# Seven edge tiles beside six node groups in a round of stage 1, and a ring of seven edge buffers

## The reference, cut to what matters

```python
# x: 50000 nodes x 256, float32; src, dst: 12500 edges, dst ascending; edge_attr: 12500 x 256
h   = relu(layernorm(x))
agg = zeros.at[dst].add(relu(h[src] + edge_attr))     # sum over the edges of a node
t   = (h + agg) @ W1 + b1                             # 256 -> 512
t   = batchnorm over the 50000 nodes, relu, @ W2      # 512 -> 256
...                                                   # two normalisations over all nodes
x   = x + (h + relu(...))
h   = relu(layernorm(x))
x   = x + relu(h @ W + segment_sum((h @ M)[src], dst))
```

## Time and profile before

| | us | what it is |
|---|---|---|
| median of three runs | 2451.24 | 2449.91 to 2452.41 |
| span of the profiled execution | 2446.4 | first to last instruction |
| PE busy | 2354.5 | 96% of the span |
| DVE busy | 2052.5 | 84% |
| ACT busy | 1713.3 | 70% |
| POOL busy | 1708.5 | 70% |
| stage 1 | 0 to 438 | first load of stage 2 issued at 438.44 |

### The profile page before, as it was taken

The page is one execution under the profiler, slowest core; times in us unless marked ns, Lnnn a source line. Parts: engine busy times, 40 slices in busy tenths (PEclk is TensorE's granted clock), DMA queues, the critical chain, the costliest instruction groups (busy, mean ns, idle before and its releaser), DMA issues. The chain is left out here.

```text
span 2446.4 us, 48745 instructions
## 1 busy us (share of the span) xinstructions
PE 2354.5 (96%) x12271; PEld 2013.5 (82%) x12271; DVE 2052.5 (84%) x5707; ACT 1713.3 (70%) x3449; POOL 1708.5 (70%) x1599
## 2 busy tenths in 40 slices
PE   7999998799999999999999999979999999989997
PEld 6888886588888888888888888858989888969996
DVE  8999997598888888888888888967777777749996
ACT  6999997466666666666666666638888888846664
POOL 5777777577767667767766666717777777767774
PEclk8999999899999999999999999999999999999999
DMA  8888995323444444444444344349999999765662
GB/s 257 283 278 275 278 277 170 124 58 127 152 150 158 163 151 147 146 146 166 153 147 145 145 164 154 141 173 405 405 411 413 413 413 413 294 197 162 173 177 88
DMA packets 242978, 531.73 MB, mean 217 GB/s; under 512 B 53856, under 2 KB 141177, under 8 KB 231442
## 3 DMA queue, kind: packets, MB, share of 16 engines
q1 hardware_dynamic: 182434, 459.36, 51.2%
q0 software_dynamic: 59808, 70.24, 10.2%
q10 hardware_dynamic: 592, 0.54, 0.1%
HBM read 340.23 MB, written 286.84 MB: 256 GB/s over the span
## 5 line engine op out<-in xcount | busy, mean ns | idle before, releaser
L1020 POOL DMA_INDIRECT ar<-sum_table,idx x392 | 462.3, 1179 | 177.6 <-issue 96.5
L1067 ACT ACTIVATE r<-pair,bnC,bnA 128x512 f32<-128x512 f32 x392 | 305.9, 781 | 380.2 <-PE pair L1268 377.7
L1471 POOL DMA_INDIRECT x1d_table<-x1r,slot x392 | 383.8, 979 | 139.8 <-issue 123.9
L1175 DVE CAST rH<-r 128x512 fp32r<-128x512 f32 x392 | 391.0, 997 | 97.7 <-ACT r L1067 97.7
L1694 PE MATMUL pair<-Ws,h1T 128*128 128x256 f32 x1568 | 358.7, 382 | 8.9 <-DVE orr L1602 7.4
L1694 PEld LDWEIGHTS pair<-Ws,h1T 128*128 128x128 f32 x1568 | 290.2, 190 | 52.1 <-issue 14.3
L1284 PE MATMUL bank<-rH,W2h 128*128 128x512 f32 (+1 forms) x784 | 305.6, 390 | 1.8 <-ACT yr L1081 1.8
L1284 PE MATMUL bank<-rL,W2h 128*128 128x512 f32 (+1 forms) x784 | 305.7, 390 | 0.0
L1284 PE MATMUL bank<-rH,W2l 128*128 128x512 f32 (+1 forms) x784 | 305.0, 389 | 0.0
L836 PE MATMUL bank<-hr 128*128 128x257 f32 (+1 forms) x1568 | 274.2, 329 | 9.6 <-ACT hr L535 9.6
L1184 DVE TENSOR_TENSOR rL<-r,rH 128x512 fp32r<-128x512 f32 x392 | 271.1, 691 | 13.5
(11 more groups left out here) (239 smaller groups left out, 5234.1 us busy)
## 6 DMA issues: line engine op xcount, KB each, us to landing
xr<-in_x SPq DMA_DIRECT2D x186, 512.0 KB, 3.9
xy_kept<-xy_table SPq DMA_DIRECT2D x57, 1024.0 KB, 20.7
x_table<-x1r SPq DMA_DIRECT2D x97, 512.0 KB, 19.8
out<-orr SPq DMA_DIRECT2D x97, 512.0 KB
xy_table<-xr SPq DMA_DIRECT2D x89, 512.0 KB, 2.6
xy_table<-yr SPq DMA_DIRECT2D x89, 512.0 KB, 3.3
xyr<-xy_table SPq DMA_DIRECT2D x32, 1024.0 KB, 21.0
sum_table<-e_tot SPq DMA_DIRECT2D x99, 128.0 KB, 4.5
```

The source lines that it names most:

```text
L1020: pool.indirect_dma_start(ar[0:p, s, j, :], None, sum_table[:, :], bass.IndirectOffsetOnAxis(ap=idx[0:p, s, j:j + 1], axis=0), bounds_chec ...
L1067: act.activation(r32[:, m, 0:n], z_ps[m][:, 0:n], ACT.Relu, bias=bnC[:, m:m + 1], scale=bnA[:, m:m + 1]).then_inc(r_kept, 1)
L1175: dve.tensor_copy(rH[:, s, m, 0:n], r32[:, m, 0:n]).then_inc(rh_kept, 1)
L1471: pool.indirect_dma_start(x1d_table[:, :], bass.IndirectOffsetOnAxis(ap=slot[0:p, part, s * T + j:s * T + j + 1], axis=0), x1r[0:p, s, j, ...
```

## The change

A round holds seven steps instead of six. The first six have a group and an edge tile, the seventh an edge tile alone. The number of rounds follows from the tiles, 99 // 7 = 14, instead of from the groups. Every ring of edge buffers and of their semaphores has seven places instead of six, as EU sets them all. Group buffers, AHEAD, the parts of the steps and their instructions are as before.

```diff
-GU, EU = 6, 6
-EH = EU // 2
+GU, EU = 6, 7

 def mixed_rounds(eng, group, edge, group_flush, edge_flush):
     def one_round(i):
-        for u in range(GU):
-            group(back((i * GU + u, u, i, GU), -AHEAD))
+        for u in range(EU):
+            if u < GU:
+                group(back((i * GU + u, u, i, GU), -AHEAD))
             edge((i * EU + u, u, i, EU))

-    full = NG // GU
+    full = ET // EU
     for i in range(2):
         one_round(i)
     with eng.Fori(2, full - 2) as i:
```

## The result

| | before | after |
|---|---|---|
| median of four runs, us | 2451.23 (2449.91 to 2452.41) | 2471.67 (2470.11 to 2472.93) |
| ratio after / before | | 1.0082, 95% interval 1.0068 to 1.0097 |
| span of the profiled execution, us | 2446.4 | 2470.7 |

The change costs 20.4 us; 15.5 were forecast. The stages after the first are the same length in both profiles, within 0.7 us: stage 2 starts at 438.44 us before and 463.45 after, 25.0 us later, and the spans differ by 24.3. In the runs whose own time is known, the span is about 1.7 us shorter than that time. So the profiled execution before took about 3 us less than its median and the one after 0.7 more, and some 4 us of the 25 belong to the two executions and not to the change.

The account below looks back on a forecast made before the run. The prediction took POOL's full list of tile DMAs to bound stage 1, with groups hidden beside it. Eight groups left on PE end stage 1 15.5 us later: 2451.24 + 15.5 = 2466.7 us, range 2459 to 2473.

Parts of the forecast that it names:

- the third rival: Stage 1: gathers take up to 7.4 us (+3.3) or the ring gives no head start (+4.0); 2470 to 2471 us, chance 0.13.
- POOL's list is full and nearly independent of the round: POOL in stage 1: goes from tile to tile without a stop, 4.025 us a tile, before and after the change.
- The other engines wait for it once a round: Rounds of stage 1: POOL needs 28.2 us, the others 26.5; DVE waits for a gather about once a round, roughly 1.7 us.
- the short step: Seventh step of a round, a tile without a group: costs DVE 2.28 us.
- Eight groups are left on PE behind tile 97: End of stage 1: PE still has groups 90 to 97 to multiply; last edge part at 449.7 instead of 434.2 us.
- Tile 97 at 416.2 us: End of the 14th round: tile 97's gather is issued at 412.1 us and lands 4.1 us later.
- The way of its gather: From POOL's issue of tile 97's gather to its landing: 4.1 us, bounds -1.3 to +3.3 us.
- The head start of the ring: POOL's wait for ACT's first finished tile moves before tile 7, still ending at 48.14 us; the list ends 4.03 us earlier.
- the pace: POOL's time per tile in stage 1: 4.025 us, between 3.97 and 4.03; -5 to 0 us over 91 tiles.
- The granted clock: PE at 440 to 444 us: a clock of 1.0 instead of 0.57 would bring -1.7 to 0 us; taken as 0.
- The rival that is not slower: Stage 1: the other engines set the pace, seven tiles every 26.5 us; change worth -1.5 us, 2449.7 us, chance 0.07.
- The rival by the port rule: Stage 1: POOL gets faster when DVE is less busy, 3.97 us a tile, list 5 us shorter; 2461.7 us, chance 0.10.

Follow-up runs that it names:

- the kernel with POOL out of the way: Changed kernel without POOL's third DMA of each tile (the scatter of edge numbers): 2449.98 us, against 2434.59 for the kernel before with the same part left out.
- the second profile: The changed kernel run once more, unaltered, beside the kernel before: 2472.54 us against 2449.07, 23.5 us slower, ratio 1.0096.
- The lead of fourteen: Changed kernel with the groups fourteen ahead instead of nine (AHEAD = 14): 2468.19 us, ratio 1.0081.
- the lightened kernel: Kernel before without POOL's third DMA of each tile (the scatter of edge numbers): 2434.59 us, one run; last edge part at 430.5 us.
- the twelve places: Order of before, steps written out, twelve places for the gathered rows and six for all else: 2444.75 us, ratio 0.9981 to the kernel before.
- their written-out base: Kernel before with all steps of stage 1 written out, no hardware loop, ring of six: 2453.28 us, ratio 1.0010 to the kernel before.
- Order of before, ring 7: Kernel before with stage 1 written out and the ring of seven alone, one group and one tile a step: 2448.40 us, ratio 0.9990.
- Order of after, ring 6: Stage 1 written out, seven tiles to six groups but still the ring of six: 2474.76 us, ratio 1.0104 to the kernel before.

## Why the prediction was right, and where it was off

- **Where the measured time fell.** The 2471.67 us lie in the stated range, 2459 to 2473, but above the 2463 to 2469 that the forecast was given. The range reaches so far only because of the third rival, so that the time lies in it is in part luck. The mechanism, groups left behind POOL's list, held; one term of the sum, the time of tile 97, did not.
- **POOL's list is full and nearly independent of the round.** Right: busy 15.51 and 15.41 of 20 us, and no wait to speak of but the one for the release. Its pace, though, came out above the upper bound of 4.03 us, as told below.
- **The other engines wait for it once a round.** Right, nine times in 240 us. The wait is 0.8 us instead of 1.7. Most of the difference is that a round of the others takes 27.2 us and not 26.5, by the kernel with POOL out of the way: the short step was put at 2.28 us, DVE's busy time in it, and it costs 2.9. That it is a chain through four engines would explain it; no run shows that.
- **Eight groups are left on PE behind tile 97.** Right, and it is the greater part of the loss: the stretch after tile 97 grew by 19.0 of the 25.0 us between the two profiles, and by 18.7 of 21.4 with the second profile. The end after tile 97 was put at 33.5 us (416.2 to 449.7) and took 34.3 and 33.9. The lead of fourteen shows it from the other side, 13.8 us less for five groups less.
- **Tile 97 at 416.2 us.** This is the term that was mis-sized: 424.9 us, and 421.7 in the second profile. The way of its gather was right or nearly so (4.1 was taken; 4.3 and 4.7 us). The head start of the ring was put at 4.03 us. In the order of before it is 4.06, but in the changed kernel tile 7 was released at 51.62 and 50.34 us, not 48.1, because DVE got a load of x, and with it ACT's first tile, later; why the load was late stays open. And the pace was 4.084 and 4.058 us a tile instead of 4.025. (From the start of tile 6 to that of tile 98 the kernel before has 4.029.) By the second profile the last gather is 4.9 us later than forecast and the end of stage 1 5.9. The sum is then 21.4 instead of 15.5 us, between the measured 20.4 and the 23.5 of the second comparison.
- **The granted clock.** The term was rightly put at 0: in the 4 us at the same place, 465 to 469 us, the changed kernel was granted 0.60 where the kernel before had 0.57.
- **The rival that is not slower** (the others set the pace, POOL follows them; then 2449.7 us) falls twice. POOL did not get faster beside the new rounds, and with a third of its work gone the change still costs 13.7 us. The rival's sum had the end right but tile 98 too early, 403.2 us: with POOL out of the way DVE reached it at 414.42. Tile 14 stood at 89.51 instead of 85.6 us, and the twelve rounds from there took 27.1 us each instead of 26.5.
- **The rival by the port rule** (POOL faster beside a less busy DVE) falls: DVE is busy 18.66 instead of 19.91 us of 20, and the gathers are longer, 1.070 and 1.061 us against 1.014 and 1.038, while the scatter, 1.036 against 1.061, is shorter by less. The Trainium skill ("SBUF — State Buffer", section "SBUF: two separate sides") gives a way in which DVE can hold POOL up; nothing in this stage shows that it does, and no run tried it with other VectorE operations.
- **The later release**, the third rival (2470 to 2471 us), is nearest to the result. Of its two conditions the gathers' way was not met; the other, a ring that gives no head start, nearly was. Tile 7 would have started at 48.14 + 4.03 = 52.17 us without the seventh place, so the ring gave 0.5 and 1.8 us of its 4.03. The pace, 3 to 5 us, stood in no rival.
- **What bounds stage 1 before** was told too simply. POOL's list does end last, but by some 4 to 6 us only (3.7 by the lightened kernel, 6.3 by the twelve places against their written-out base, 429.77 against 436.04); the ten tiles behind the groups are nearly as late by themselves. For this change it made no difference, for a better kernel it does: relief of the list alone stops paying there.

## What to carry to other kernels

Of two kinds of work in one pipeline, the one with the short step should be what is left at the end: here the end after tile 97 takes 14 to 16 us with tiles alone and 34 to 35 with groups among them. A finer balance in the rounds gained nothing here, as a list outside them set their pace, and it took work away from where it was hidden. Before evening out two streams, write down what stands on each engine after the last item of the slowest one.

## What was not expected of the hardware

The same indirect DMA instructions on POOL have other durations in the two orders. Order of before, ring 7, from 54 to 420 us:

```profile
L437 POOL DMA_INDIRECT id_table<-index,spot x91 | 97.5, 1071 | 27.7 <-issue 26.8 <-ACT e_hd L568 0.6 <-DMA id_table<-index,spot 0.3
L428 POOL DMA_INDIRECT e_s<-in_x,index x90 | 93.5, 1039 | 27.4 <-issue 27.1 <-ACT e_hd L568 0.3
L431 POOL DMA_INDIRECT e_d<-in_x,index x91 | 92.2, 1013 | 27.9 <-issue 27.3 <-ACT e_hd L568 0.6
```

Order of after, ring 6:

```profile
L433 POOL DMA_INDIRECT e_s<-in_x,index x90 | 96.0, 1067 | 27.5 <-issue 27.2 <-ACT e_hd L573 0.3
L436 POOL DMA_INDIRECT e_d<-in_x,index x91 | 94.5, 1038 | 27.9 <-issue 27.0 <-ACT e_hd L573 0.9
L442 POOL DMA_INDIRECT id_table<-index,spot x91 | 93.5, 1028 | 27.8 <-issue 21.0 <-ACT e_hd L573 6.7
```

The gathers grow by 0.03 us each, the scatters shrink by 0.04. The sum moves by 0.01 us a tile here, and by 0.03 to 0.05 in the changed kernel. DMA moves 248 instead of 278 GB/s at 200 to 220 us of these two traces. No run tells the cause.
